# A relational graph layer's masks, walked by quarter instead of by source tile

## The reference, cut to what matters

```
for l in range(2):
    transformed = einsum('nbi,rbio->rnbo', h.reshape(N, 8, 12), weights[l]).reshape(8, N, 96)
    msg = transformed[etype, src] * edge_norm            # 1 / in-degree of dst
    agg = segment_sum(msg, dst, num_segments=N)
    h_new = agg + h @ loop_w[l] + bias[l]
    h = relu(h_new) if l < 1 else h_new
```

## Time and profile before

| what | value |
|---|---|
| median of 3 runs | 2676.79 us (2673.07, 2676.79, 2677.56) |
| profiled execution | 2674.12 us, its span 2672.5 us |
| mean granted TensorE clock | 0.943 |
| table stage, layer 0 and 1 | ends at 1720.46 and 2134.40 us |
| product stage, layer 0 and 1 | 1721.8 to 2082.3, 2135.7 to 2496.2 us |

### The profile page before, as it was taken

The page is one execution under the profiler, slowest core; times in us unless marked ns, Lnnn a source line. Parts: engine busy times, 40 slices in busy tenths (PEclk is TensorE's granted clock), DMA queues, the critical chain, the costliest instruction groups (busy, mean ns, idle before and its releaser), DMA issues. The chain is left out here.

```text
span 2672.5 us, 63273 instructions
## 1 busy us (share of the span) xinstructions
PE 2358.1 (88%) x21713; PEld 1750.1 (65%) x21714; DVE 2196.8 (82%) x4727; ACT 1221.1 (46%) x2285; POOL 530.3 (20%) x936
## 2 busy tenths in 40 slices
PE   3999999799999999678776786899999899999897
PEld 1555555599999999211111112599999599999787
DVE  8999999855655665699999998699888689888645
ACT  2888888632323332699999997400000400000223
POOL 1111111000000000100000000266665066656000
PEclk9999999899999999787889887899999999999899
DMA  2333333301100100511111112422222422222620
GB/s 65 132 141 120 141 134 127 143 27 39 38 27 26 38 26 1 134 38 38 36 38 38 38 38 74 154 83 82 71 82 42 185 69 82 75 77 57 224 93 19
DMA packets 95193, 206.50 MB, mean 77 GB/s; under 512 B 21620, under 2 KB 61172, under 8 KB 94880
## 3 DMA queue, kind: packets, MB, share of 16 engines
q1 hardware_dynamic: 80544, 182.38, 19.6%
q0 software_dynamic: 14464, 21.44, 4.4%
HBM read 118.17 MB, written 84.76 MB: 76 GB/s over the span
## 5 line engine op out<-in xcount | busy, mean ns | idle before, releaser
L1807 PE MATMUL l_bank<-tab,mask 128*128 128x192 f16 x7600 | 652.5, 247 | 38.4 <-issue 29.7
L1807 PEld LDWEIGHTS l_bank<-tab,mask 128*128 128x128 f16 x7600 | 629.0, 98 | 57.7 <-issue 56.3
L1395 DVE TENSOR_SCALAR mask<-code 128x1600 int32<-128x1600 int32 x304 | 538.2, 1811 | 77.3 <-remote 40.5
L1779 POOL DMA_INDIRECT ggot<-table_dram,gidx x432 | 410.3, 950 | 241.0 <-issue 85.3
L1277 DVE SCALAR_TENSOR_TENSOR pr<-ex,cring 128x1568 f32<-128x1568 f32 x200 | 355.3, 1777 | 13.4 <-DMA cring<-c_dram 9.7
L1204 PE MATMUL score<-qa,ka 96*128 (+1 forms) x800 | 233.1, 392 | 140.7 <-DVE least L1270 123.1
L1204 PEld LDWEIGHTS score<-qa,ka 96*128 96x128 f16 x800 | 55.0, 104 | 378.5 <-DVE least L1270 179.6
L816 PE MATMUL sums<-onehots,ct 128*128 128x192 f16 x3125 | 267.8, 250 | 14.5 <-issue 8.3
L816 PEld LDWEIGHTS sums<-onehots,ct 128*128 128x128 f16 x3125 | 264.3, 99 | 17.9 <-issue 11.6
L816 PE MATMUL sums<-u,ct 128*128 128x192 f16 x3125 | 259.1, 246 | 0.0
L816 PEld LDWEIGHTS sums<-u,ct 128*128 128x128 f16 x3125 | 258.0, 98 | 0.0
(11 more groups left out here) (341 smaller groups left out, 2656.3 us busy)
## 6 DMA issues: line engine op xcount, KB each, us to landing
code<-code_dram SPq DMA_DIRECT2D x38, 800.0 KB
code_dram<-flat SPq DMA_DIRECT2D x100, 200.0 KB, 1.9
ct_dram<-ct SPq DMA_DIRECT2D x25, 800.0 KB, 3.6
c_dram<-flat SPq DMA_DIRECT2D x25, 800.0 KB, 3.3
ct_again<-ct_dram SPq DMA_DIRECT2D x25, 800.0 KB, 16.8
cring<-c_dram SPq DMA_DIRECT2D x200, 98.0 KB, 1.9
table_dram<-tab SPq DMA_DIRECT2D x50, 384.0 KB, 2.3
flat<-code_dram SPq DMA_DIRECT2D x19, 800.0 KB, 4.3
```

The source lines that it names most:

```text
L1395: e.tensor_scalar(turned.rearrange("p (s q d) -> p s q d", q=NQ, d=DQ // 2), words.rearrange("p (q s d) -> p s q d", q=NQ, d=DQ // 2), abs ...
L1779: e.indirect_dma_start(ggot[:, k, j, :], None, table_dram[:, :], bass.IndirectOffsetOnAxis(ap=gidx[:, k, j:j + 1], axis=0)).then_inc(s_ggo ...
L1807: mm = e.matmul(acc[k][:, 0:2 * D], mask[:, r % MR, s, :], tab[:, s, r, :], start=(r == 0 and s == 0), stop=(r == R - 1 and s == NT - 1))
```

## The change

The loop order of the one instruction that makes a mask. Source words lie as [q, s, d], mask words as [s, q, d], d being 16 32-bit words. Before, both sides are walked s, q, d; after, both are walked q, s, d. The same words go to the same places, by the same instruction count.

```
                     words = code[:, t % SLOTS, :, :, :].rearrange("p q s d -> p (q s d)").bitcast(I32)
-                    e.tensor_scalar(turned.rearrange("p (s q d) -> p s q d", q=NQ, d=DQ // 2),
-                                    words.rearrange("p (q s d) -> p s q d", q=NQ, d=DQ // 2), abs(up), 0x0C000C00,
+                    e.tensor_scalar(turned.rearrange("p (s q d) -> p q s d", q=NQ, d=DQ // 2),
+                                    words.rearrange("p (q s d) -> p q s d", q=NQ, d=DQ // 2), abs(up), 0x0C000C00,
                                     ALU.logical_shift_left if up >= 0 else ALU.logical_shift_right,
                                     ALU.bitwise_and).then_inc(s_mask, 1)
```

## The result

The changed kernel is **slower**: 2715.31 us median of four runs (2703.11 to 2718.29) against 2674.93 for the kernel before beside it; ratio 1.0143, 95% interval 1.0108 to 1.0178. The forecast was 2671.2. The profiled execution took 2717.57 us, 43.45 more than that of before.

What follows compares the result with a forecast made beforehand. The prediction took TensorE to bound the product stages, with VectorE close behind. Gains of 3.78 and 1.78 us, 5.56 in all, off the median of 2676.79 gave 2671.2 us, range 2660 to 2679.

Steps and rivals of the forecast that it cites:

- Part 1: The mask instruction on VectorE: the new walk qualifies for the fast speed, 985 ns in place of 1811.
- Part 2: Table stages: faster masks no longer push back VectorE's half tiles and so TensorE's tile starts; gain 3.78 us.
- Part 3: Around tile 1's end, where TensorE runs out of masks in both layers: those waits go; gain 1.78 us.
- Part 4: Rest of the product stages: 296 masks lie beside TensorE's work, so their 243 us of savings count nothing.
- The first rival: Product stages: more of TensorE's idle gaps were mask waits; a third of 31 us closing gives 2660.9; chance 0.13.
- The third rival: Product stages: fast masks shut GpSimd out and stretch its gathers, making the kernel slower, 2720 to 2879 us; chance 0.12.
- The rule that masks and whole gathers take turns: Product stages: each blocks the other throughout, a layer needing 405 us, 2731 in all; a third of 0.12.

Runs made afterwards that it cites:

- fast_in_table: Kernel before, with the new walk only for the four masks of each layer made in the table stage; 2672.27 us, ratio 0.9984.
- old_walk_padded: Kernel before with its old walk, but 4 unused columns behind each mask row of 128; 2695.98 us, ratio 1.0069.
- after_filled: Changed kernel with a VectorE reduction of 740 elements behind each mask of the product stages; 2695.68 us, ratio 1.0062.
- half_masks: Kernel before with its slow walk, but masks after the first four compute only 13 of 25 source tiles; 2675.62 us, ratio 0.9996.

## Why the prediction was wrong

**Part 1** was right: 985 ns forecast, 994 the median (973 at least).

**Part 2** was right: fast_in_table gave 4.3 us (1.9 to 6.7) for 3.78. TensorE's tile starts in the table stages of the changed kernel are 1.45 us apart where the masks stand, but for two steps of 1.52 and 1.55 us in layer 1.

**Part 3** was right as far as it shows. In time its 1.78 us are too small to be told alone: with tiles 1 and 2 added the gain was 5.8 (3.4 to 8.1) for the 5.56 of parts 2 and 3. In the trace, where 0.63 and 0.34 us stood, the changed kernel has no gap:
```profile
1757.89 1.15 PE L1813 MATMUL l_bank<-ggot,goh 128*128 128x192 f16 x12
1758.88 7.34 PE L1807 MATMUL l_bank<-tab,mask 128*128 128x192 f16 x87
```

**Part 4 failed.** "What is late next is TensorE itself" was the false step. It priced the 296 masks by what VectorE gains, nothing, and left what they do to a neighbour to a rival at 0.12. What is late next is GpSimd. Its gathers went from 950 to 1305 ns, and to 1351 without gaps; there its work alone takes 383.1 and 384.6 us a stage where TensorE needs 335.5. The first rival (more gaps were masks) got nothing: without gathers the change gave 3 to 7 us, as much as parts 2 and 3 say.

**The third rival** had the mechanism, and both its sizes were off. Its mean stretch, "0.2 us in the mean", took mask and gather for strangers that meet by chance, and thought that only the end of a gather is shut out. They fall into step, since a held gather restarts 2.11 us after a mask's start and masks come every 2.06, and a gather that starts under a mask ends 0.82 us after it. The mean stretch was 0.355 us with gaps, 0.40 without. Its threshold, 0.42 to 0.50 us, counted 1.25 us for each of 216 gathers and let GpSimd use up its lead of 16.7 us. But the changes of group cost 19 us, not 17 steps of 0.30, the stage begins 5 us ahead of the first gather, and the last group has to be there at the end. By the sum above it is (360.5 - 92)/216 = 1.243, a stretch of 0.29 us, and 0.18 without gaps. With 0.20 against 0.29 the rival would still have looked unlikely, but narrowly. With the right stretch, of 0.355, the sum gives 27 us for both stages and 3.8 come off in the table stages, about 2700 us in all: slower, as measured, but 15 us short of the 2715.31.

The rule that masks and whole gathers take turns, priced at 2731 and given a third of 0.12, was the nearer, and is half right: a gather waits for a whole mask, while a mask is held by only a part of a gather, and then for 0.16 us in the mean. The Trainium skill, "SBUF — State Buffer", section "Who interferes with whom", says that one blocks the other for the whole instruction. The traces agree for a gather under a mask (begun 0.05 us into a mask of 0.99 us it took 1.76 for 0.94), not for a mask under a gather. They add that a row of instructions can block on, for 4.28 us.

**What stays open.** In the runs with gaps, those that the forecast was made for, the sum gives only 27 of the 47.9 us, and TensorE's waits for gathered rows come to 6. The changed kernel's stages should take 376.7 and 371.0 us by it and took 386.7 and 382.1; old_walk_padded should take 360.5, TensorE's own time there, and took 372.3 and 372.8, with GpSimd well ahead. (after_filled should take 361.5 and 367.9 and took 377.6 and 369.7, so the rest is 16 us there in one stage and 2 in the other.) Of the changed kernel's 10 and 11 us about half can be the lower clock; old_walk_padded, at 0.99 in both stages, has the rest without it. It stands as more "issue", in stretches like this one of weight loads in the changed kernel:
```profile
1878.38 0.45 PEld L1807 LDWEIGHTS l_bank<-tab,mask 128*128 128x128 f16 x6 [0.36 <-issue]
1879.12 0.36 PEld L1807 LDWEIGHTS l_bank<-tab,mask 128*128 128x128 f16 x5 [0.29 <-issue]
1879.86 0.28 PEld L1807 LDWEIGHTS l_bank<-tab,mask 128*128 128x128 f16 x4 [0.38 <-issue]
```
Before weight loads of the products "issue" comes to 88.6 us in the changed kernel, 78.3 in old_walk_padded and 67.7 in after_filled, but 54.0 in half_masks and 57.4 in fast_in_table, with slow masks in these stages. So fast masks add to TensorE's gaps there by a way that I can't name. Whether that too needs the gathers is open: no run without gathers, and no split mask, met that condition.

## What to carry to other kernels

Before making a VectorE instruction fast, write down the sum of GpSimd's work beside it, group changes, head and tail included. Then ask when a held instruction starts again: if that is about one period of the fast instructions, count every meeting, not the chance of one. A release that the profile names can be a chance event; look up what the instruction really waits for, and whether its idle time is longer than without a wait. Where the margin is thin, make the fast instruction in pieces, or fast only where VectorE is late. Both kept the gain here: 2620.50 us with the new walk up to tile 2, and 2624.84 with split masks, against 2627.5 to 2629.8 before and 2716 after.

## What I had not expected

A gather of 0.94 us can be held for 4.28 us by four fast instructions in a row, while one mask cut in two lets it in at the cut. A gather and a mask that wait for nothing in common fell into step by their lengths alone. And the same kernel, even on one chip, took 2676 or 2628 us in different groups of runs; nearly all of it was "issue" time of TensorE before weight loads (56.3 against 8.1 us) in stages that are full of instructions, so a kernel's margin on a second engine has to be counted against the shorter time.
